# Ranking two sort keys on TensorE, and five smaller changes, in a graph network with experts

## What is computed

```python
# layer 0, node = src, edge = dst
alpha = leaky_relu(sum(concat(xh[node], eh[edge]) * att), 0.2)
alpha = exp(alpha - segment_max(alpha, node)); alpha /= segment_sum(alpha, node)
out_e = segment_sum(Binv[edge] * alpha * xh[node], edge)
out_n = segment_sum(Dinv[node] * alpha * out_e[edge], node)
x = layernorm(x + out_n)
# layer 1
h = x * rsqrt(deg_out);  m = segment_sum(h[src], dst) * rsqrt(deg_in)
x3 = m @ W_gc + b_gc + x @ W_res + b_res
y = x3 + top2_experts(x3)          # gelu(x3 @ w1 + b1) @ w2 + b2, gated
x = layernorm(x + batchnorm(y))
```

## Time and profile before

| | us |
|---|---|
| runs of the kernel (three) | 8351.1, 8670.9, 8798.5 |
| median | 8670.9 |
| profiled execution | 8481.7 |
| its span, first to last instruction | 8480.1 |
| busy in the span: PE, DVE, ACT, POOL | 3725, 4656, 2015, 4494 |

### The profile page before, as it was taken

How to read it: one execution, slowest core, us unless ns; L and a number is a source line. 1 busy time by engine, 2 the same in 40 slices (tenths; PEclk the granted TensorE clock), 3 DMA queues, 4 the chain that set the end, 5 groups by cost and what they waited for, 6 DMA issues and landing times. The chain is left out here.

```text
span 8480.1 us, 95762 instructions
## 1 busy us (share of the span) xinstructions
PE 3725.3 (44%) x18399; PEld 2408.2 (28%) x18399; DVE 4655.9 (55%) x8209; ACT 2014.7 (24%) x3817; POOL 4494.3 (53%) x4044
## 2 busy tenths in 40 slices
PE   0000011666633313346555554255555570788820
PEld 0000001233210000024444443133333360666620
DVE  8969201999989939965555556522222242111127
ACT  0000000222279939931111111000000021222201
POOL 1888776577767750036666664466677604000042
PEclk9999999999966656667777776566666685999965
DMA  0000000111111100036666666533333501777731
GB/s 14 5 6 5 6 7 10 37 40 40 40 55 28 28 10 29 28 55 83 83 82 83 83 83 80 192 88 88 88 88 89 84 4 59 223 236 236 236 114 45
DMA packets 363085, 612.29 MB, mean 72 GB/s; under 512 B 101120, under 2 KB 233157, under 8 KB 363044
## 3 DMA queue, kind: packets, MB, share of 16 engines
q0 software_dynamic: 159536, 295.77, 19.1%
q1 hardware_dynamic: 196308, 284.10, 10.6%
q10 hardware_dynamic: 7200, 32.03, 0.9%
HBM read 506.74 MB, written 104.90 MB: 72 GB/s over the span
## 5 line engine op out<-in xcount | busy, mean ns | idle before, releaser
L909 POOL DMA_INDIRECT rowsS<-hyperedge_rows,idxS x928 | 992.4, 1069 | 1118.6 <-issue 855.1
L1240 POOL DMA_INDIRECT rows<-h_table,idx x928 | 963.7, 1038 | 571.2 <-DVE idx L1274 318.2
L248 POOL DMA_INDIRECT slots_by_source<-spay,sidx x833 | 1016.0, 1220 | 426.5 <-issue 253.4
L1258 PE MATMUL pm<-rows,ohT 128*128 128x257 f32 x1856 | 721.7, 552 | 822.0 <-issue 336.0
L103 POOL DMA_INDIRECT slots_by_target<-pay,slot_int x833 | 910.0, 1092 | 264.5 <-issue 239.3
L831 PE MATMUL OE<-Pb,xs 128*32 128x512 f32 (+1 forms) x2352 | 410.8, 863 | 893.5 <-DVE xs L695 714.8
L1258 PEld LDWEIGHTS pm<-rows,ohT 128*128 128x128 f32 x1856 | 482.1, 276 | 1061.3 <-issue 975.6
L541 PE MATMUL running<-onehot_edge,onehot_node 128*128 128x512 bf16 (+1 forms) x2784 | 595.7, 362 | 258.3 <-SPq L478 90.5
L676 DVE SCALAR_TENSOR_TENSOR Pb<-negative_b,ai,low 128x1251 f32<-128x1251 f32 x392 | 585.1, 1512 | 168.9 <-remote 153.2
L962 PE MATMUL pmS<-rowsS,ohS 128*128 128x256 f32 x1856 | 650.4, 514 | 9.8 <-DVE rowsS L1077 9.8
L317 PE MATMUL pX<-W,xT 128*128 128x256 f32 x236 | 120.6, 666 | 1181.3 <-ACT xT L265 1170.6
(11 more groups left out here) (281 smaller groups left out, 6665.8 us busy)
## 6 DMA issues: line engine op xcount, KB each, us to landing
w<-in_L_gnn_w_dram SPq DMA_DIRECT2D x322, 512.0 KB
negative_log_counts<-log_counts ACTq DMA_DIRECT2D x49, 625.5 KB
log_counts_in<-negative_log_counts SPq DMA_DIRECT2D x49, 625.5 KB
expert_inputs<-zeroE SPq DMA_DIRECT2D x23, 896.0 KB
xt<-expert_inputs SPq DMA_DIRECT2D x161, 128.0 KB
expert_outputs<-ye POOLq DMA_DIRECT2D x161, 128.0 KB, 4.5
rowsS<-hyperedge_rows,idxS POOLq DMA_INDIRECT x928
rows<-h_table,idx POOLq DMA_INDIRECT x928
```

Source lines behind the costliest of these rows:

```text
L248: pool.indirect_dma_start(k.SS[:, :], bass.IndirectOffsetOnAxis(ap=sidx[:, u, c:c + 1], axis=0), spay[:, u, c, :], None, bounds_check=boun ...
L909: pool.indirect_dma_start(rows[:, u, q, :], None, k.OEB[:, :], bass.IndirectOffsetOnAxis(ap=idx[:, u, q:q + 1], axis=0), bounds_check=boun ...
L1240: pool.indirect_dma_start(rows[:, u, q, 0:FEAT], None, k.H[:, :], bass.IndirectOffsetOnAxis(ap=idx[:, u, q:q + 1], axis=0), bounds_check=b ...
L1258: last = pe.matmul(pm[:, (u % 2) * (Q // 2) + g, 0:FEAT + 1], oh[:, u, q, :], rows[:, u, q, :], start=(q % 2 == 0), stop=(q % 2 == 1))
```

## The change

It has six parts.

1. `phase_rank` comes before `phase_project`. Both keys are ranked in it with f16 one-hots, one comparison of 832 columns for each bucket. TensorE sums the columns of each bucket over the partitions (`T`), DVE scans them, adds the bases, splits the offsets in two f16 parts, and for each bucket TensorE computes the slots as a product with a strictly upper triangle plus the offsets (`V`). DVE picks them by `copy_predicated`. An edge list of 830 columns of 128, and 10 edges more, takes the place of rows of 833.
2. The source edges are scattered in `phase_project` by the same helper as the targets, straight from the tiles of slots and payloads, 831 columns. The logits of seven tiles follow as soon as these are projected.
3. In the count POOL's `mask` goes. ScalarE negates the logarithm and stores it, and POOL adds the mask of the empty pairs to it in DRAM by a DMA with `accum_op=ALU.add`. POOL scatters 7 target columns to a bucket instead of 6.
4. In the softmax POOL scatters 5 columns for each half bucket and waits for `s_pm` between.
5. In both gather phases all 928 columns of indices are made at once, POOL's loop is unrolled and waits for TensorE's sums, DVE reads the bucket numbers ahead of its wait, and in phase_messages_back the additions of a step move behind the exponents of the next, ScalarE's copies of the bucket rows ahead of its exponential.
6. In the experts the rows are turned two tiles ahead on a semaphore of their own, and `b2` is split into three bf16 rows beforehand, so that the bias is one bf16 product with three rows.

The semaphores of the first five phases are allocated apart, and cleared and freed behind them, with one more barrier of all engines.

```diff
+def phase_rank(nc, k):                     # tensor
+            for j in range(2):
+                for b in range(NTILE):
+                    pe.wait_ge(s_eq, j * NTILE + b + 1)
+                    for c, w in halves:
+                        last = pe.matmul(T[0:ROWS, c:c + w], column[:, NTILE - 1 - b:NTILE - 1 - b + ROWS], eq[b][:, c:c + w],
+                                         start=(b == 0), stop=(b == NTILE - 1))
+                last.then_inc(s_T, 1)
...
+                for b in range(NTILE):
+                    n = j * NTILE + b
+                    if n >= 2:
+                        pe.wait_ge(s_cp, n - 1)
+                    for c, w in halves:
+                        v = V[:, n % 2, c:c + w]
+                        pe.matmul(v, upper16[:, :], eq[b][:, c:c + w], start=True, stop=False)
+                        last = pe.matmul(v, sel[:, b, :], offp[:, c:c + w], start=False, stop=True)
+                    last.then_inc(s_v, 1)
...
+                                            # vector
+                for b in range(NTILE):
+                    dve.tensor_scalar(eq[b], bucket[:, :], float(b), None, ALU.is_equal).then_inc(s_eq, 1)
...
+                for b in range(NTILE):
+                    n = j * NTILE + b
+                    dve.wait_ge(s_v, n + 1)
+                    if b >= 2:
+                        dve.wait_ge(s_cp, n - 1)
+                    dve.copy_predicated(slotf[:, b % 2, :], eq[b].bitcast(I16), V[:, n % 2, 0:ECOL]).then_inc(s_cp, 1)
...
                                             # phase_project, gpsimd
+            scatter = k.sources.on(pool)
+            scatter.columns(0, ECOLS)
+            scatter.finish()
...
                                             # phase_count, gpsimd and scalar
-            def mask(b):
+            def join(b):
                 pool.wait_ge(s_ln, b * 2 + 2)
-                pool.tensor_tensor(lc[:, b % 2, :], none[:, b % 2, :], lc[:, b % 2, :], ALU.subtract).then_inc(s_neg, 1)
+                pool.wait_ge(s_LC[b % 2], 16 * (b // 2) + 16)
+                pool.dma_start(k.LC[b, :, :], none[:, b % 2, :], accum_op=ALU.add).then_inc(s_join[b % 2], 16)
...
+                act.activation(lc[:, u, :], lc[:, u, :], ACT.Copy, scale=-1.0).then_inc(s_neg, 1)
...
                                             # phase_softmax, gpsimd
-            scatter.columns(EARLY, ECOL)
+            for h in range(2 * NTILE):
+                if h:
+                    pool.wait_ge(s_pm, h + 2)
+                first = min(EARLY + h * HALVES, ECOLS)
+                scatter.columns(first, min(first + HALVES, ECOLS))
             scatter.finish()
...
                                             # phase_gather, gpsimd (phase_messages_back alike)
-            with pool.Fori(0, NI // B) as i:
-                for u in range(B):
-                    pool.wait_ge(s_idx, i * B + u + 1)
+            pool.wait_ge(s_idx, 1)
+            for n in range(NI):
+                if n >= B:
+                    pool.wait_ge(s_mm, (n - B) * (Q // 2) + Q // 2)
...
                                             # phase_experts, tensor
-                pe.matmul(pY[:, u, 0:FEAT], k.ones[0:1, :], b2[:, w, :], start=True, stop=False)
                 pe.wait_ge(s_g, t + 3)
                 pe.sem_inc(idle["pe"], 1)
+                pe.matmul(pY[:, u, 0:FEAT], ones3[:, :], b2[:, w, :], start=True, stop=False)
...
+            def step(t, u, i, turning, hiding):
+                if turning:
+                    turn(t + 2, (u + 2) % B, i * 16 + (32 if u + 2 >= B else 16))
+                if hiding:
+                    hidden(t + 1, (u + 1) % B, i * 48 + (96 if u + 1 >= B else 48))
+                outputs(t, u)
```

More of the change, by code:

```diff
@@ L79, with __init__ @@
     pass
-PER = 6
+PER = 7
+HALVES = 5
 EARLY = PER * NTILE
-class TargetScatter:
-    def __init__(self, k, done):
-        self.k, self.done = k, done
+class EdgeScatter:
+    def __init__(self, table, slot, pay, done):
+        self.table, self.slot, self.pay, self.done = table, slot, pay, done
         self.landed, self.n = [0, 0], 0
@@ L1009, in _ @@
             act.wait_ge(s_u3, 1)
-            copy(0, 0)
-            copy(1, 1)
+            for u in range(2):
+                buckets(u, u)
+                copy(u, u)
             exp(0, 0)
             def step(n, u, left):
+                if left > 2:
+                    buckets(n + 2, u + 2)
                 if left > 1:
@@ L1091, in _, with step, last @@
             weigh(0, 0)
[L1093 to L1094 removed]
+            exponents(1, 1, 16 * Q)
+            weigh(1, 1)
+            def step(n, u, gathered, more):
+                at = buckets(n - 1)
+                dve.wait_ge(s_mm, n * (Q // 2))
+                dve.sem_inc(idle["dve"], 1)
+                prepare(n + B - 1, u + B - 1)
+                if more:
                     exponents(n + 1, u + 1, gathered)
+                add(n - 1, u - 1, at)
+                if more:
                     weigh(n + 1, u + 1)
[L1097 to L1102 removed]
+            def last(n, u, gathered):
+                at = buckets(n - 1)
+                dve.wait_ge(s_mm, n * (Q // 2))
+                dve.sem_inc(idle["dve"], 1)
+                if n + 1 < NI:
+                    exponents(n + 1, u + 1, gathered)
+                add(n - 1, u - 1, at)
+                if n + 1 < NI:
+                    weigh(n + 1, u + 1)
             with dve.Fori(0, NI // B - 1) as i:
                 o.enter(i, 3 * B)
[L1105 to L1106 removed]
+                for u in range(1, B + 1):
+                    step(i * B + u, u, i * (16 * Q) + (32 if u + 1 >= B else 16) * Q, True)
                 o.leave(NI // B - 1)
[L1108 to L1109 removed]
+            for u in range(1, B + 1):
+                last(NI - B + u, u, 16 * Q * (NI // B))
             dve.wait_ge(s_add, NI * (Q // 2) + Q)
@@ L1803, in _ @@
             rows(0, 0)
-            with dve.Fori(0, MT // B) as i:
+            rows(1, 1)
+            with dve.Fori(0, MT // B - 1) as i:
                 for u in range(B):
-                    rows(i * B + u + 1, u + 1)
+                    rows(i * B + u + 2, u)
                     outputs(i * B + u, u)
-            outputs(MT - 1, 0)
+            for t in range(MT // B * B - B, MT):
+                if t + 2 < MT:
+                    rows(t + 2, t)
+                outputs(t, t)
         @block.gpsimd
@@ L2081, in gnn_resnorm_kernel @@
         k.big2 = sb("big2", [P, NTILE, FEAT + 1], F32)
[L2082 removed]
+        for phase in PHASES[5:]:
             phase(nc, k)
```

571 lines of the change are left out of this document (307 added, 264 removed).

## The result

| | before | after |
|---|---|---|
| runs | 8351.1, 8464.4, 8670.9, 8798.5 | 7837.2, 7840.6, 7848.0, 7902.7 |
| median | 8567.6 | 7844.3 |
| profiled execution | 8481.7 | 7840.6 |
| ratio, 95% interval | | 0.9345 [0.9214, 0.9477] |

The forecast was 7530 us. The direction was right and the time fell into the range, but the change gave 6.5% where I had worked out 13.2% against the median, 11.2% against the profiled execution. The runs of before spread over 447 us, those of after over 65; that turned out to be part of the answer.

A forecast was written before the change was run, and what follows sets the result against it. Stages run one after another, each with its own limit (POOL, DVE, PE or stores). Six stage estimates plus 882 us untouched gave 7484; with 42 us of gather waits kept, the forecast was 7530 us, range 7380 to 7860.

The forecast's parts named there:

- Waits of 422 us are said to vanish wholly in the two gathers; I let a tenth stay: Way back and gather: POOL's waits for indices go, bar 42 us; stages 1581 to 1322 and 1419 to 1250 us.
- (a): Softmax: the stall stays, being PE's own and not POOL's; 7677 us, up to 7980; chance 0.17.
- (b): Both gather stages: gathers follow a chain through DVE, ScalarE and PE; half of 422 us stays, 7700; chance 0.1.
- Softmax 1155 for 1163: Softmax: pacing POOL's scatters ends DVE's stall, 1317 to 1163 us; least certain term, between 154 us gained and nothing.
- Experts 810 for 828: Experts: rows turned ahead and a cheaper bias bring a tile from 5.51 to 4.9 us, the stage from 920 to 828.
- rival (d): Experts: stores land quicker and PE sets 4.45 us a tile; 7458 us in all; chance 0.15.
- Rival (c): Experts: the store chain keeps its 5.5 us a tile; 7627 us in all; chance 0.3.
- 831 x 1.27: Projection: POOL scatters 831 columns at 1.27 us each, 1055 us, for a stage of 1076.
- PE: 18 tiles x 0.58: Count: PE needs 10.4 us a bucket plus some 2.5 for the copy of counts, against 14.0 for DVE.
- the 133: Count: dropping POOL's second operation saves 49 DVE stalls of 2.7 us, 133 us, 861 to 728.
- The issue of the adding DMA: Count: 0.54 up to 2.7 us on POOL; from 2.1 POOL sets the bucket, at worst 29 us; nothing taken.
- The base: Whole kernel: spread of runs before, median 8670.9, lowest 8351, read as the 147 us softmax stall; sum not scaled.

The follow-up runs named there:

- X: Kind of chip, not a kernel: those where the kernel before had medians of 8341, 8354 and 8943 us; the prediction's runs are of this kind.
- Y: Kind of chip, not a kernel: those where the kernel before had medians of 7970 and 7983 us.
- a paced before: Kernel before, with POOL scattering six softmax columns per half bucket and waiting for PE between; ratio to before 1.0006 twice on Y, 0.9981 on X.
- experiment 5: Kernel after with eight instead of four buffered steps in both gather stages and four expert output buffers instead of two; 7751 us beside 7878 for after.
- experiment 6: Kernel after with DVE's hardware loop in the gather stage written out; 7901 us in a single run, gather stage 1361 for 1362 with the loop.
- one-go form: Kernel after with POOL issuing the softmax's 488 columns without waiting for PE's half buckets; 7588 and 7625 us on Y, 7864 on X.

## Why the prediction missed

The step that failed is the one on the waits in the two gather stages, "Waits of 422 us are said to vanish wholly in the two gathers; I let a tenth stay". On X 106 and 64 us went, 170 in all, and on Y, where the old loop has hardly any, 0 and 7. The second step that failed is the size of PE's period in the count. That the time fell into the range is no credit to the working: the range took in rivals (a) and (b), and the time came near its upper end.

- **Stages that hold.** Softmax 1155 for 1163, and as the prediction had it, pacing ends the stall on X, in both kernels. The 162 us are luck all the same: the profiled execution of before had 147 us of stall, on Y there was none, and a paced before gained 0.2% in the median. Ranking 204 for 235. Experts 810 for 828, and the chain of stores as the limit, as argued against rival (d); experiment 5 bears it out. Rival (c), 5.5 us a tile, fell.
- **Projection, "831 x 1.27".** On Y it is near: 0.991 us a scatter (823.39/831) and 0.3 between two, 1.29, and a stage of 1079 for 1076. On X a scatter takes 1.060 on the mean. I took the pace of the quiet second stretch of the earlier trace rows, whose maximum is 0.987, for the whole; in the first stretch of the same row it went up to 6.98. +65.
- **Count, "PE: 18 tiles x 0.58".** A mis-sized term. The earlier trace rows gave 2.31 us for four tiles; I left out the 0.50 of idleness behind each four and took 18 tiles for 18.9. The stop at each copy, 1.74, was in the sum with 2.5. With 928/49 = 18.9 tiles, 18.9 x 0.70 + 1.7 = 15.0 us a bucket, and the copies of the counts come every 15.3 (1382.2 to 2117.2 us, 49 of them): 735 us, and 73 for start and end. I took PE's 12.9 as under DVE's 14.0, and it is over it. DVE's stalls went as I had said (its 853 us became 681); 75 us of the 133 came through on Y. The issue of the adding DMA is 1.04 us, inside the bounds, and its wait costs nothing, as I had said.
- **Gathers, "waits of 422 us are said to vanish wholly; I let a tenth stay".** The step that carried most of the miss, 258 of some 350 us. The waits were real on X and their places right, but I read them as the form of the loop. On Y the old loop has next to none of them (14 and 29 us), and POOL is at its 1.41 and 1.33 us a gather already. On X the new loop takes away 106 and 64 us, and then the pace is set by sums that come late: neither deeper buffers nor a cheaper POOL nor quicker register work on DVE moves it. What makes them late on X stays open. That is rival (b), at a chance of 0.1 and priced at half of the waits; two fifths of them went (170 of 422). 33 us of the way back are the gather's own price, 1.105 on Y and 1.124 on X for my 1.069: on Y the old loop, which doesn't wait either, has 1.103 (1023.35/928). On X it was 1.019 us without DVE's multiplication beside it and 1.137 with. The Trainium skill (SBUF — State Buffer, Who interferes with whom) says that a DVE instruction with two SBUF inputs contends with a GpSimd instruction that reads SBUF. The two numbers agree with it, but no run here tells whether a port is the reason.
- **The base.** I didn't scale the sum though the runs of before were spread from 8351 to 8798, and read the spread as the softmax's stall alone. That spread said that a part of what I was about to remove comes and goes.

## What to carry to other kernels

Before a wait is booked as gain, ask whether the code needs it: a wait without a named cause ("issue", "remote"), in a kernel whose runs spread by 5%, may belong to the chip or its state. When the bound engine gets faster, price the next one by its whole period, idle gaps of its own making included, not by its busy time. A buffer count is a test: if doubling it changes nothing, the average pace of one engine is the limit. And what looks slow in a trace is the limit only if the stage gets shorter without it: the short instructions of experiment 6 weren't.

## What I had not expected of the hardware

- Five chips gave the same kernel 7970 to 8943 us. The new kernel was less sensitive: 7831 to 7878 on X, and 7588 and 7625 on Y, in the one-go form.
- A scatter by POOL takes 0.991 us (823.39/831) on Y and 1.060 on X with the same work beside it, and a gather with all other engines idle took 1.065 us (987.99/928) on X, more than the 1.040 (964.80/928) beside working ones.
- Register instructions of up to 1396 ns in a hardware loop on X took 33 at most in straight code on the same chip, and the stage took as long.
- Seven indirect scatters without a break, in place of three and four around a short wait, came with a count 240 us longer on X.
- A DMA that adds 625.5 KB into DRAM takes POOL 1.04 us to issue (51.2 us in 49), and its traffic (81 GB/s for 40 in the count) slowed nothing that can be seen: on Y the count took 792 us with it and 793 without.
